# A four-stage residual chain on one core: n2 of blocks 1 to 6 turned in 32x32 squares by VectorE and moved by DMA, L3 two steps back

## The chip, the core and the metric

The kernel runs on one core of a Trainium2 chip: TensorE (matmul), VectorE, ScalarE, GpSimd and the sync engine SP, which issues nearly all DMAs. A core has SBUF (128 partitions) and PSUM (8 banks of 128 x 512 fp32, here pt 0 and 1, pc 0 and 1, pm 0 to 3). The metric is device time in microseconds.

## The reference

x is (2, 2048, 512) fp32. Four layers follow each other; the weights of the last three are picked by an index for each of the two sequences. Cut to what matters:

```python
# L0: gated traces, then a layer norm, residual
ctx = causal_ema(x, tau_ctx)
gated = x * sigmoid([x, ctx] @ Wg.T + bg)
...
n = layernorm((gelu(x @ Wsoma.T) * sigmoid(temporal @ Wtemp.T)) @ Wout.T) * gamma + beta
y = x + n
# L1: residual linear, per sequence
x2 = y + (y @ W[cat] + b)
# L2: adapter, then a layer norm, residual
x2' = x2 + relu(x2 @ W1[lang] + b1) @ W2[lang] + b2
x3 = x2 + layernorm(x2') * gamma2 + beta2
# L3: per-subject linear
out = x3 @ weight[subj].T + bias[subj]
```

## The kernel before, in words

The 4096 tokens are cut into 8 blocks of 512 (NBLK = 8, LAST = 7; blocks 0 to 3 are sequence 0, 4 to 7 sequence 1). Activations are mostly held channels by tokens, as 4 chunks (NC) of 128 x 512. fp32 products are made of three fp32r matmuls of a high and a low part (product(), L609 to L611), so each activation that enters a product is written twice: the high part by ScalarE (x_h, s_h, t_h, h_h), the rest by VectorE (x_l, s_l, t_l, h_l).

The first half of the time runs L0 over the 8 blocks; its normalised output n goes to n_scratch in DRAM, x to xt_scratch. There 16-bit pieces are transposed by DMA into x_pairs and put in order by four DMAs of 256 KB, x_pairs to x_planes (spread(), L290). The second half runs L1 to L3. A step step2(i) on TensorE (from L896), with nothing but the order of the code and semaphores as its plan:

- l1_product(i, m), m = 0 to 3: 12 matmuls each into pc; m = 2 needs x2_hi and x2_lo of m = 0 (the bank), m = 3 those of m = 1.
- inside m = 1 and m = 2 lie turn_n2(i-1): 16 transposes of stage_a (128x128, four fill a bank, turn(), L616), from tokens by channels into pt, channels by tokens.
- in steps 5 and 6 turn_y(i+1), 16 transposes of x_pairs.
- l3_product(i-1, k), k = 0 to 3: L3 of the block before, 12 matmuls each; w1_product(i) behind k = 0, xx_product(i) (4 tiles: x2 turned by 4 transposes, and 3 matmuls of the adapter) behind k = 2, k = 3 last.

What the other engines do for block i: ScalarE x2_parts (s_h and x_t from pc), relu_part, normalise of tiles 0 and 1 into stage_a, x2_beta (soma = x_t + beta_b2), x3_hi_part (t_h), y_hi_part (x_h). VectorE x2_lo_part (s_l, L1601), norm2_stats (L1632, L1635), normalise of tiles 2 and 3 (L1640), x3_sum_part (gate = n2 * gamma + soma from PSUM, L1610), x3_lo_part (t_l, L1616), y_sum_part (L1453), y_lo_part (x_l, L1594), hid_lo_part (L1621), output (L1628). GpSimd norm2_scale: rstd and nbias from the statistics (L503 to L519), and the low parts of two weights. SP load_y (n half into x_pairs, L392, xt half into ctx_t, L396) and store_out (L410). SP and each engine run strictly in order.

The names the prediction's steps touch: step2 and last_step2 on TensorE, l1_product, turn_n2, l3_bank, n2_bank; between the halves hid_lo_part(0), xx_product(0), turn_l3(1, k) and subject_lo(1, k) (wt_l, L1589), which make the L3 weights of sequence 1.

Of the kernel before, what the change touches and what calls it, by code (L numbers as in the profile page):

```python
# [5 lines left out]
P = 128  # L6
# [16 lines left out]
def residual_chain_kernel(nc: bass.Bass, t: dict, out: bass.AP):  # L23
# [23 lines left out]
    with ExitStack() as ctx:  # L47
# [3 lines left out]
        def sem(name):  # L51
# [106 lines left out]
        (y_hi, x2_hi, x2_all, relu_done, hid_hi, n2_act, n2_dve, x3_hi) = (  # L158
            sem(n) for n in ("y_hi", "x2_hi", "x2_all", "relu_done", "hid_hi", "n2_act", "n2_dve", "x3_hi"))
# [24 lines left out]
        l2_raw = [mod[:, :, :], stage_b[:, 0:2, :]]  # L184
# [10 lines left out]
        def x2_parts_of(i):  # L195

            return (t_h, t_l) if isinstance(i, int) and i == 0 else (s_h, s_l)
# [41 lines left out]
        def last_block(j):  # L239
            return isinstance(j, int) and j == LAST  # L240
# [4 lines left out]
        def first_block(j):  # L245
            return isinstance(j, int) and j == 0

        def n2_bank(j, c):
            if last_block(j):
                return [pc[0], pc[1], pt[1], pt[0]][c]  # L250
            return [pt[0], pt[1], pm[2], pm[3]][c] if first_block(j) else pt[c % 2]

        def l1_bank(i, m):

            return pc[(m + 1) % 2] if isinstance(i, int) and i == 1 else pc[m % 2]

        def l3_bank(j, k):
            if isinstance(j, int) and j == NBLK - 2:
                return [pm[0], pm[1], pt[1], pt[0]][k]
            return [pm[0], pm[1], pm[2], pm[3] if last_block(j) else pt[0]][k]  # L260
# [6 lines left out]
        def _(sp):  # L267
# [130 lines left out]
            def load_y(i):  # L398

                sp.wait_ge(y_sum, i * NC)  # L400
# [50 lines left out]
            load_l1_half(1, 1)  # L451
            store_n(LAST)
# [6 lines left out]
            def second_l2():  # L459
                sp.wait_ge(l3_turned, 2 * NC)  # L460
                load_l2(1)

            def store_block(j):
# [17 lines left out]
        def _(pool):  # L481
# [103 lines left out]
            def adapter_lo(b):  # L585
                for n, (raw, wh, wl) in enumerate(adapter_parts(b)):
# [17 lines left out]
        def _(pe):  # L604
# [209 lines left out]
            def l1_product(i, b, m, between=None):  # L814
# [14 lines left out]
                if between:  # L829
                    between()  # L830
# [953 lines left out]
```

## Time and profile before

| | |
|---|---|
| median of 3 runs | 757.39 us (757.36 to 757.73) |
| the profiled execution, its own time | 755.23 us |
| its span, first to last instruction | 753.3 us |
| instructions | 10450 |
| ScalarE busy | 366.7 us, 49% |
| GpSimd busy | 113.4 us, 15% |
| TensorE weight loads (beside matmuls) | 606.2 us, 80% |
| granted TensorE clock | 0.999 of full |
| DMA traffic | 86.17 MB, mean 114 GB/s |

Lines of the trace's timeline have: start in us, duration in us, engine, line of the kernel, operation, output <- inputs, shapes, count, and in brackets the idle time of the engine before it with what ended it. Matmuls are pipelined: a 128x512 matmul shows 0.39 us, but the next starts 0.23 later; the distance of starts is the price. The steps step2(i) lie from about 513 us to the end.

### The profile page before, as it was taken

What the parts mean: (1) busy time and instruction counts of PE and PEld (TensorE: products, weight loads), DVE (VectorE), ACT (ScalarE), POOL (GpSimd) and SP (SyncE); (2) the same over time, 40 slices, a digit from 0 to 9 for tenths busy, and PEclk for the clock granted to TensorE, in tenths of its full rate; (3) what the DMA queues carried; (4) which work ended last, traced back from release to release, by engine and by line L of the source; (5) the groups of instructions that cost most, each with busy time, mean ns of one, the idle gap of its engine ahead of it and who ended that gap; (6) DMA issues with size and microseconds to landing.
All of it is one profiled execution on the core that took longest, in us unless ns stands there. A gap on an engine that the chain in (4) does not pass through costs nothing. (4 is left out here: it accounts for less than half of the span.)

```text
span 753.3 us, 10450 instructions
## 1 busy us (share of the span) xinstructions
PE 743.6 (99%) x3421; PEld 606.2 (80%) x3421; DVE 534.3 (71%) x786; ACT 366.7 (49%) x550; POOL 113.4 (15%) x222
## 2 busy tenths in 40 slices
PE   7999999999999999999999999999999999999997
PEld 6888888888888888888888788878888888888885
DVE  4598895695695595597587579866867767666645
ACT  5363346445535535535536543656564553636331
POOL 2000040031022013004004024114301021010110
PEclk9999999999999999999999999999999999999999
DMA  8964007916934953962971872526143131331002
GB/s 267 222 180 45 28 1 110 195 59 97 188 78 79 189 95 65 185 111 54 169 139 31 138 223 73 207 85 220 56 157 138 57 127 55 129 107 74 28 33 80
DMA packets 93020, 86.17 MB, mean 114 GB/s; under 512 B 61583, under 2 KB 75950, under 8 KB 90942
## 3 DMA queue, kind: packets, MB, share of 16 engines
q1 hardware_dynamic: 91614, 81.57, 45.2%
q10 hardware_dynamic: 1184, 4.23, 1.7%
q8 instruction: 15, 0.25, 0.1%
q0 software_dynamic: 192, 0.00, 0.1%
q14 instruction: 15, 0.12, 0.1%
HBM read 33.33 MB, written 25.20 MB: 78 GB/s over the span
## 5 line engine op out<-in xcount | busy, mean ns | idle before, releaser
L609 PE MATMUL pc<-x_h,wg_h 128*128 128x512 f32 x224 | 88.8, 396 | 0.0
L611 PE MATMUL pc<-x_h,wg_l 128*128 128x512 f32 x224 | 88.1, 393 | 0.0
L610 PE MATMUL pc<-x_l,wg_h 128*128 128x512 f32 x224 | 87.7, 391 | 0.0
L1421 DVE TENSOR_TENSOR_SCAN stage_b<-alpha,carry,stage_b 128x512 f32<-128x512 f32 x64 | 78.5, 1268 | 0.0
L1100 ACT ACTIVATE ctx_t<-ctx_t,col_all 128x512 f32<-128x512 f32 x32 | 23.1, 723 | 57.1 <-DVE ctx_t L1401 57.1
L609 PE MATMUL pm<-wo_h,s_h 128*128 128x512 f32 x128 | 50.7, 396 | 0.0
L611 PE MATMUL pm<-wo_h,s_l 128*128 128x512 f32 x128 | 50.6, 395 | 0.0
L610 PE MATMUL pm<-wo_l,s_h 128*128 128x512 f32 x128 | 50.6, 395 | 0.0
L726 PE MATMUL pm<-t_h,wt_l 128*128 128x512 f32 x128 | 50.6, 395 | 0.0
L724 PE MATMUL pm<-t_h,wt_h 128*128 128x512 f32 x128 | 50.5, 395 | 0.0
L725 PE MATMUL pm<-t_l,wt_h 128*128 128x512 f32 x128 | 50.3, 393 | 0.0
L609 PEld LDWEIGHTS pc<-x_h,wg_h 128*128 128x128 f32 x224 | 42.2, 188 | 9.8 <-issue 0.6
L611 PEld LDWEIGHTS pc<-x_h,wg_l 128*128 128x128 f32 x224 | 42.1, 188 | 9.4
L610 PEld LDWEIGHTS pc<-x_l,wg_h 128*128 128x128 f32 x224 | 42.1, 188 | 9.1
L503 POOL TENSOR_TENSOR newton<-mv,const 128x4 f32<-128x4 f32 x16 | 9.6, 600 | 251.5 <-DVE mv L1635 181.1
L1415 DVE SCALAR_TENSOR_TENSOR stage_b<-mod,w_blend,ctx_t 128x512 f32<-128x512 f32 x64 | 45.7, 756 | 2.4 <-DVE ctx_t L1405 1.5
L1374 DVE SCALAR_TENSOR_TENSOR gate<-gate,soma 128x512 f32<-128x512 f32 x32 | 21.9, 698 | 35.6 <-ACT gate L1055 35.6
L1106 ACT ACTIVATE t_h<-stage_b 128x512 fp32r<-128x512 f32 x32 | 20.4, 636 | 47.9 <-DVE stage_b L1428 47.7
L1055 ACT ACTIVATE gate<-pm,col_all 128x512 f32<-128x512 f32 x32 | 21.6, 688 | 45.2 <-PE pm L726 29.9
L1256 ACT ACTIVATE stage_a<-pm,nbias,rstd 128x512 f32<-128x512 f32 x16 | 11.6, 775 | 55.9 <-POOL nbias L519 55.8
L1601 DVE SCALAR_TENSOR_TENSOR s_l<-pc,seq_b,s_h 128x512 fp32r<-128x512 f32 x28 | 21.0, 750 | 24.0 <-ACT x_t L1231 24.0
L611 PE MATMUL pc<-x_h,ws_l 128*128 128x512 f32 x96 | 38.0, 396 | 0.0
(245 smaller groups left out, 1932.7 us busy)
## 6 DMA issues: line engine op xcount, KB each, us to landing
x_planes<-x_pairs SPq DMA_DIRECT2D x52, 256.0 KB, 7.4
xt_scratch<-x_t SPq DMA_DIRECT2D x8, 1024.0 KB, 10.3
n_scratch<-stage_a SPq DMA_DIRECT2D x8, 1024.0 KB, 10.1
ctx_t<-xt_scratch SPq DMA_DIRECT2D x16, 512.0 KB, 6.3
x_pairs<-n_scratch SPq DMA_DIRECT2D x14, 512.0 KB, 5.3
out_dram<-x_tok SPq DMA_DIRECT2D x28, 256.0 KB, 2.0
mod<-mod_scratch ACTq DMA_DIRECT2D x8, 512.0 KB, 3.8
stage_b<-in_L_cond_weight_dram SPq DMA_DIRECT2D x2, 1024.0 KB, 5.5
```

The costliest lines, as they stand in the source:

```text
L609: nc.tensor.matmul(acc, ah, bh, start=start and q == 0, stop=False)
L610: nc.tensor.matmul(acc, ah, bl, start=False, stop=False)
L611: last = nc.tensor.matmul(acc, al, bh, start=False, stop=stop and q == n - 1)
L724: nc.tensor.matmul(pm[m][:, :], wt_h[:, c, o], t_h[:, c, :], start=(c == 0), stop=False)
L725: nc.tensor.matmul(pm[m][:, :], wt_h[:, c, o], t_l[:, c, :], start=False, stop=False)
L726: last = nc.tensor.matmul(pm[m][:, :], wt_l[:, c, o], t_h[:, c, :], start=False, stop=(c == NC - 1))
L1055: nc.scalar.activation(gate[:, m % 2, :], pm[m][:, :], ACT.Tanh, bias=cols["btemp"][:, m:m + 1], scale=0.5).then_inc(gate_t, 1)
L1100: nc.scalar.activation(ctx_t[:, m, :], ctx_t[:, m, :], ACT.Tanh, bias=cols["bg"][:, m:m + 1], scale=0.5).then_inc(z_t, 1)
L1374: nc.vector.scalar_tensor_tensor(gate[:, m % 2, :], gate[:, m % 2, :], 1.0, soma[:, m, :], ALU.add, ALU.mult).then_inc(s_prod, 1)
L1415: nc.vector.scalar_tensor_tensor(tr[:, m % 2, :], mod[:, d, :], w_blend[:, d, m:m + 1], ctx_t[:, m, :], ALU.mult, ALU.mult).then_inc(prods, 1)
L1421: nc.vector.tensor_tensor_scan(tr[:, m % 2, :], alpha[:, 1 + d:2 + d].to_broadcast([P, BLK]), tr[:, m % 2, :], carry[:, D - d, m:m + 1], A ...
L1601: nc.vector.scalar_tensor_tensor(c_l[:, m, :], l1_bank(i, m)[:, :], seq["b1"][:, b, m:m + 1], f32(c_h[:, m, :]), ALU.add, ALU.subtract).th ...
```

## The change

n2 of blocks 1 to 6 is no longer transposed by TensorE. ScalarE normalises all four tiles of such a block into stage_a, VectorE transposes 32x32 squares within each (turn_squares) into stage_b, SP moves the squares by 16 DMAs of 64 KB between groups of 32 partitions into x_planes (move_n2), ScalarE applies gamma and beta and puts the columns in order (scale_n2), VectorE adds x2 (x3_sum_part). That takes longer from end to end, so L3 of block j runs in step j + 2 and not j + 1, with other banks; x2 alternates between x_t and soma, and x2_beta goes. Blocks 0 and 7 are still turned by TensorE. Step 1 and step 2 are written out on their own, the tail (last_blocks) has L3 of block 6 around turn_n2(7). The loops over steps are unrolled. VectorE's order within a step is new. The load of y of block 2 comes before store_n(LAST), and VectorE sums it ahead of hid_lo(0). adapter_lo(1) moves from GpSimd to VectorE.

```diff
+        def turned_by_pe(j):
+
+
+            return j == 0 or j == LAST
+
+        def n2_acts(j):
+
+            return 2 + 4 * j - (2 if j == LAST else 0)
...
+            def move_n2(j):
+
+                sp.wait_ge(n2_squares, j * TILES)
+                if j == 1:
+                    sp.wait_ge(x3_lo, NC)
+                else:
+                    sp.wait_ge(n2_scaled, (j - 1) * NC)
+                for q in range(4):
+                    for a in range(4):
+                        part, tok = slice(32 * a, 32 * a + 32), slice(P * a, P * a + P)
+                        sp.dma_start(x_planes[32 * q:32 * q + 32, :, tok],
+                                     squares_q[part, :, q, :]).then_inc(n2_in, 16)
...
+            second_l3()
+            sp.wait_ge(s_lo, NBLK * NC)
+            load_l2(1)
+            store_out(0, 0)
+            load_y(3)
+            store_out(0, 1)
+            for i in range(2, NBLK):
+                move_n2(i - 1)
+                if i == 2:
+                    load_y(4)
+                    store_out(0, 2)
+                    store_out(0, 3)
+                    continue
+                store_out(i - 2, 0)
+                store_out(i - 2, 1)
+                if i + 2 < NBLK:
+                    load_y(i + 2)
+                store_out(i - 2, 2)
+                store_out(i - 2, 3)
+            for j in (LAST - 1, LAST):
                 for k in range(TILES):
                     store_out(j, k)
-
-            load_y(2)
-            second_l3()
-            store_block(0)
-            second_l2()
-            with sp.Fori(2, LAST) as i:
-                load_y(i + 1)
-                store_block(i - 1)
-            store_block(LAST - 1)
-            store_block(LAST)
...
+            def second_step2():
+                for m in range(NC):
+                    if m < 2:
+                        pe.wait_ge(l3_hi, 2 * NC)
+                        pe.wait_ge(l3_lo, 2 * NC)
+                    l1_product(2, 0, m)
+                l3_tile(0, 2)
+                w1_product(2, 0)
+                l3_tile(0, 3)
+                for k in range(TILES):
+                    xx_product(2, 0, k)
+
+            def step2(i):
+                b = i // PER_SEQ
+                l1_product(i, b, 0)
+                l1_product(i, b, 1)
+                if turns_y(i):
                     turn_y(i + 1, 0)
                     turn_y(i + 1, 1)
-                if not weights:
-                    l3_product(i - 1, bp, 0)
-                    w1_product(i, b)
-                if turned:
+                l1_product(i, b, 2)
+                l1_product(i, b, 3)
+                if turns_y(i):
                     turn_y(i + 1, 2)
-                l3_product(i - 1, bp, 1)
-                if turned:
                     turn_y(i + 1, 3)
-                l3_product(i - 1, bp, 2)
-                if weights:
-                    pe.wait_ge(relu_done, i + 1)
-                    turn_l3(1, 0, pt[1])
-                    turn_l3(1, 1, pc[1])
+                l3_tile(i - 2, 0)
+                w1_product(i, b)
+                l3_tile(i - 2, 1)
+                l3_tile(i - 2, 2)
                 for k in range(TILES):
                     xx_product(i, b, k)
-                if weights:
-                    turn_l3(1, 2, pt[1])
-                    turn_l3(1, 3, pc[1])
-                l3_product(i - 1, bp, 3, turned)
-
-            def last_step2(i, b):
-                l1_product(i, b, 0)
-                l1_product(i, b, 1, lambda: turn_n2(i - 1, (0, 1)))
-                l1_product(i, b, 2, lambda: turn_n2(i - 1, (2, 3)))
-                l1_product(i, b, 3)
-                l3_product(i - 1, b, 0)
-                w1_product(i, b)
-                l3_product(i - 1, b, 1)
-                for k in range(TILES):
-                    xx_product(i, b, k)
-                pe.wait_ge(x3_sum, i * NC)
-                l3_tile(l3_bank(i - 1, 2), b, 2)
-                l3_tile(l3_bank(i - 1, 3), b, 3)
-                turn_n2(i, range(NC))
-
-                wh, wl = l3_w(b)
+                l3_tile(i - 2, 3)
+
+            def last_blocks():
+                l3_tile(LAST - 1, 0)
+                l3_tile(LAST - 1, 1)
+                turn_n2(LAST)
+                l3_tile(LAST - 1, 2)
+                l3_tile(LAST - 1, 3)
...
+            def scale_n2(j, m):
+
+                b = j // PER_SEQ
+                act.wait_ge(n2_in, j * 256)
+                nc.scalar.activation(stage_b[:, m, :].rearrange("p (k a i) -> p k a i", k=TILES, a=4),
+                                     x_planes[:, m, :].rearrange("p (a k i) -> p k a i", k=TILES, a=4), ACT.Identity,
+                                     bias=seq["beta_b2"][:, b, m:m + 1],
+                                     scale=seq["gamma2"][:, b, m:m + 1]).then_inc(n2_scaled, 1)
+
...
+            def turn_squares(j, k):
+
+                dve.wait_ge(n2_act, n2_acts(j - 1) + k + 1)
+                if j == 1:
+                    dve.wait_ge(l3_turned, 2 * NC)
                 else:
-                    x2_lo_part(i, b, 0)
-                    x3_sum_part(i - 1, bp, 0)
-                    x3_sum_part(i - 1, bp, 1)
-                    x3_lo_part(i - 1, 0)
-                    x3_lo_part(i - 1, 1)
-                    x2_lo_part(i, b, 1)
-                    x3_sum_part(i - 1, bp, 2)
-                    x3_sum_part(i - 1, bp, 3)
-                    x3_lo_part(i - 1, 2)
-                    x3_lo_part(i - 1, 3)
-                    x2_lo_part(i, b, 2)
-                    x2_lo_part(i, b, 3)
-                if not last:
-                    y_sum_part(i + 1, 0, turned)
-                    y_sum_part(i + 1, 1, turned)
-                    y_lo_part(i + 1, 0)
-                    y_lo_part(i + 1, 1)
-                output(i - 1, bp, 0)
+                    dve.wait_ge(x3_lo, j * NC)
+                nc.vector.transpose(squares[:, :, k, :], stage_a[:, k, :].rearrange("p (f i) -> p f i", i=32)
+                                    ).then_inc(n2_squares, 1)
+
+            def adapter_lo(b):
+                for n, (raw, wh, wl) in enumerate(adapter_parts(b)):
+                    dve.wait_ge(l2_hi, b * 2 + n + 1)
+                    nc.vector.tensor_tensor(wl, raw, f32(wh), ALU.subtract).then_inc(l2_lo, 1)
+
+            def step2(i):
+                j = i - 2
+                turned, more = turns_y(i), i < LAST
+                if j >= 1:
+                    for m in range(NC):
+                        x3_lo_part(j, m)
+                x2_lo_part(i, 0)
+                turn_squares(i - 1, 0)
+                if more and not turned:
+                    y_sum_part(i + 1, 0)
+                x2_lo_part(i, 1)
+                if more and not turned:
+                    y_sum_part(i + 1, 1)
+                    y_sum_part(i + 1, 2)
+                if turned:
+                    y_sum_part(i + 1, 0, True)
+                    y_sum_part(i + 1, 1, True)
+                turn_squares(i - 1, 1)
+                turn_squares(i - 1, 2)
+                x2_lo_part(i, 2)
+                turn_squares(i - 1, 3)
+                if more and not turned:
+                    y_sum_part(i + 1, 3)
+                x2_lo_part(i, 3)
+                if turned:
+                    y_sum_part(i + 1, 2, True)
+                    y_sum_part(i + 1, 3, True)
+                if more:
+                    for c in range(NC):
+                        y_lo_part(i + 1, c)
+                output(j, 2 if j == 0 else 0)
                 hid_lo_part(i)
-                if not last:
-                    y_sum_part(i + 1, 2, turned)
-                output(i - 1, bp, 1)
-                if not last:
-                    y_sum_part(i + 1, 3, turned)
-                    y_lo_part(i + 1, 2)
-                    y_lo_part(i + 1, 3)
-                    output(i - 1, bp, 2)
-                if weights:
-                    subject_lo(1, 0, pt[1])
-                    subject_lo(1, 1, pc[1])
+                output(j, 3 if j == 0 else 1)
+                if i == LAST:
+                    for m in range(NC):
+                        x3_sum_part(i - 1, m)
+                if j > 0:
+                    output(j, 2)
                 for k in range(TILES):
                     norm2_stats(i, k)
-                if weights:
-                    subject_lo(1, 2, pt[1])
-                    subject_lo(1, 3, pc[1])
-                if last:
-                    output(i - 1, bp, 2)
+                if i < LAST:
+                    for m in range(NC):
+                        x3_sum_part(i - 1, m)
                 else:
-                    output(i - 1, bp, 3)
-                normalise(i, 2)
-                normalise(i, 3)
-                if last:
-                    output(i - 1, bp, 3)
+                    for m in range(NC):
+                        x3_lo_part(i - 1, m)
+                if j > 0:
+                    output(j, 3)
 
...
+            for c in range(3):
+                y_sum_part(2, c)
             hid_lo_part(0)
```

## Rows read from the trace of the kernel before

**Rows 1.** Page, part 1: busy time, share of span, instructions.
```profile
PE 743.6 (99%) x3421; PEld 606.2 (80%) x3421; DVE 534.3 (71%) x786; ACT 366.7 (49%) x550; POOL 113.4 (15%) x222
```

**Rows 2.** TensorE's waits, whole span: us in total, times, longest.
```profile
PE pm L959 <- DVE t_l L1616: 1.1, 1, 1.1
```

**Rows 3.** Stretches: length, busy us by engine, TensorE clock, DMA share, GB/s.
```profile
611.50:642.80 31.30, 31.30 (x154) 25.77 (x153) 22.72 (x36) 15.70 (x25) 4.88 (x11) 1.00 0.29 99
642.80:675.85 33.05, 33.05 (x171) 27.41 (x170) 22.22 (x37) 15.42 (x24) 2.47 (x9) 1.00 0.27 99
```

**Rows 4.** Timeline of TensorE around one pair of n2 quads.
```profile
642.01 1.03 PE L616 MATMUL pt<-ident,stage_a 128*128 128x128 f32 x8
642.80 0.48 PE L609 MATMUL pc<-x_h,wo_h 128*128 128x512 f32 x1
643.12 0.39 PE L610 MATMUL pc<-x_l,wo_h 128*128 128x512 f32 x1
643.35 0.40 PE L611 MATMUL pc<-x_h,wo_l 128*128 128x512 f32 x1
```

**Rows 5.** Timeline of TensorE and VectorE, block 7's n2 and L3.
```profile
735.57 1.07 PE L616 MATMUL pc<-ident,stage_a 128*128 128x128 f32 x8
...
738.65 0.47 PE L959 MATMUL pm<-wt_h,t_h 128*128 128x512 f32 x1 [1.14 <-DVE t_l L1616]
...
737.81 0.69 DVE L1616 TENSOR_TENSOR t_l<-gate,t_h 128x512 fp32r<-128x512 f32 x1 [0.17 <-ACT t_h L1243]
```

**Rows 6.** VectorE: a group by line (busy, mean ns), and a pair in time.
```profile
L1421 DVE TENSOR_TENSOR_SCAN stage_b<-alpha,carry,stage_b 128x512 f32<-128x512 f32 x64 | 78.5, 1268 | 0.0
...
524.14 1.28 DVE L1616 TENSOR_TENSOR t_l<-gate,t_h 128x512 fp32r<-128x512 f32 x2
```

**Rows 7.** Timeline: end of xx(7), last statistics on VectorE, last scale on GpSimd.
```profile
729.71 0.40 PE L609 MATMUL pt<-wt_h,t_h 128*128 128x512 f32 x1
...
730.75 0.18 DVE L1635 BATCH_NORM_AGGREGATE mv<-stats 128x2 f32<-128x6 f32 x1
...
733.66 0.20 POOL L519 TENSOR_TENSOR nbias<-newton,nbias 128x4 f32<-128x4 f32 x1
```

**Rows 8.** Timeline of a tile of l1: TensorE, ScalarE, VectorE (step 1, m = 1).
```profile
513.26 0.40 PE L609 MATMUL pc<-x_h,wg_h 128*128 128x512 f32 x1
...
516.22 0.69 ACT L1228 ACTIVATE s_h<-pc,seq_b 128x512 fp32r<-128x512 f32 x1 [2.08 <-PE pc L611]
...
517.62 0.75 DVE L1601 SCALAR_TENSOR_TENSOR s_l<-pc,seq_b,s_h 128x512 fp32r<-128x512 f32 x1 [2.46 <-ACT x_t L1231]
```

**Rows 9.** SP's issues in time, landing of x_planes, stretches during a spread.
```profile
299.51 2.61 SPq L290 DMA_DIRECT2D x_planes<-x_pairs  x4
...
310.05 4.60 SPq L284 DMA_TRANSPOSE x_pairs<-in_x_dram  x1
...
671.97 0.33 SPq L410 DMA_DIRECT2D out_dram<-x_tok  x1
...
DMA to landing us min/median/max: 4.4/7.4/9.3
...
303.00:304.00 1.00, 1.00 (x6) 0.82 (x5) 0.22 (x1) 0.69 (x2) 0.00 (x0) 1.00 1.17 123
...
310.00:311.00 1.00, 1.00 (x6) 0.51 (x5) 0.89 (x2) 0.00 (x0) 0.00 (x0) 1.00 1.03 434
```

**Rows 10.** Between the halves: SP, VectorE, TensorE; landing of ctx_t (L396).
```profile
497.21 0.95 SPq L373 DMA_DIRECT2D stage_b<-in_L_cond_W_dram  x2
...
498.18 2.73 DVE L1594 SCALAR_TENSOR_TENSOR x_l<-ctx_t,col_all,x_h 128x512 fp32r<-128x512 f32 x4
...
506.88 0.69 DVE L1621 TENSOR_TENSOR h_l<-h,h_h 128x512 fp32r<-128x512 f32 x1 [2.53 <-ACT h_h L1251]
...
508.64 0.66 PE L616 MATMUL pm<-ident,x_t 128*128 128x128 f32 x4 [0.40 <-ACT stage_a L1112]
...
DMA to landing us min/median/max: 3.8/6.3/8.3
```

More of the change, by code:

```diff
@@ L861, in xx_product @@
+                nc.tensor.matmul(pm[k][:, :], hl, wh, start=False, stop=False, skip_group_check=True)
+                nc.tensor.matmul(pm[k][:, :], hh, wl, start=False, stop=True,
                                  skip_group_check=True).then_inc(xx_mm, 1)
[L863 to L874 removed]
@@ new lines, in l3_tile @@
+            def l3_tile(j, k):
+                b = j // PER_SEQ
+                if turns_y(j + 2) and k < 3:
+                    pe.wait_ge(n2_act, n2_acts(j + 1))
+                elif turns_y(j + 2):
+                    pe.wait_ge(y_sum, (j + 3) * NC + 3)
+                elif j == LAST - 1 and k >= 2:
+                    pe.wait_ge(n2_act, n2_acts(LAST))
+                    pe.wait_ge(n2_dve, 4)
+                elif j == LAST - 1 and k == 0:
+                    pe.wait_ge(out_ready, j * TILES - 1)
+                else:
+                    after(pe, out_ready, j * TILES + max(k - 1, 0))
@@ new lines, in l3_tile, with first_step2 @@
+                for c in range(NC):
+                    if k == 0:
+                        pe.wait_ge(x3_hi, j * NC + c + 1)
+                        pe.wait_ge(x3_lo, j * NC + c + 1)
+                    last = product(l3_bank(j, k)[:, :], [(ch[:, c, tok], cl[:, c, tok], wh[:, c, :], wl[:, c, :])],
+                                   start=(c == 0), stop=(c == NC - 1))
+                last.then_inc(l3_mm, 1)
+            def first_step2():
+                for m in range(1, NC):
+                    l1_product(1, 0, m)
+                turn_n2(0)
+                w1_product(1, 0)
+                pe.wait_ge(l3_hi, NC)
+                pe.wait_ge(l3_lo, NC)
+                l3_tile(0, 0)
+                l3_tile(0, 1)
+                pe.wait_ge(relu_done, 2)
+                turn_l3(1, 0, pc[0])
+                turn_l3(1, 1, pc[1])
+                for k in range(TILES):
+                    xx_product(1, 0, k)
+                turn_l3(1, 2, pc[0])
+                turn_l3(1, 3, pc[1])
@@ new lines, in step2 @@
+            def step2(i):
+                if i >= 3:
+                    for m in range(NC):
+                        x3_hi_part(i - 2, m)
+                x2_parts(i, 0)
+                normalise(i - 1, 0)
+                x2_parts(i, 1)
+                normalise(i - 1, 1)
+                normalise(i - 1, 2)
+                x2_parts(i, 2)
+                normalise(i - 1, 3)
+                x2_parts(i, 3)
+                if i < LAST:
+                    for c in range(NC):
+                        y_hi_part(i + 1, c)
+                relu_part(i)
+                for m in range(NC):
+                    scale_n2(i - 1, m)
@@ L1313, in _ @@
             subject_hi(0, 3, pt[1])
[L1314 to L1316 removed]
+            relu_part(0)
             for k in range(TILES):
@@ new lines, in _ @@
+            x3_lo_part(0, 0)
+            x3_lo_part(0, 1)
+            x3_sum_part(0, 2)
+            x3_sum_part(0, 3)
+            x3_lo_part(0, 2)
+            x3_lo_part(0, 3)
+            hid_lo_part(1)
+            for c in range(NC):
+                y_lo_part(2, c)
+            output(0, 0)
+            output(0, 1)
+            subject_lo(1, 0, pc[0])
+            subject_lo(1, 1, pc[1])
+            for k in range(TILES):
+                norm2_stats(1, k)
+            subject_lo(1, 2, pc[0])
@@ L1747, in _ @@
+            subject_lo(1, 3, pc[1])
+            adapter_lo(1)
+            for i in range(2, NBLK):
+                step2(i)
+            normalise(LAST, 2)
+            normalise(LAST, 3)
+            output(LAST - 1, 0)
+            output(LAST - 1, 1)
+            x3_sum_part(LAST, 0)
+            x3_sum_part(LAST, 1)
             x3_lo_part(LAST, 0)
-            x3_sum_part(LAST, 1, 2)
+            x3_sum_part(LAST, 2)
             x3_lo_part(LAST, 1)
-            x3_sum_part(LAST, 1, 3)
+            x3_sum_part(LAST, 3)
```

391 lines of the change are left out of this document (158 added, 233 removed).

## Prediction, made before the change was built

> **What bounds the kernel now.** I read the totals of the page first: TensorE is busy for 99% of the span, VectorE for 71% [rows 1]. A share alone doesn't prove a bound, so TensorE's waits come next: in the second half the longest is 1.1 us, in front of the last L3 [rows 2], and the next 0.4 [rows 10]. The table of stretches then shows one step of the second half as 31.3 us, TensorE busy throughout at the full granted clock, and 33.05 us where 16 more transposes (turn_y) lie in the step [rows 3]. So in the second half every TensorE instruction that goes shortens the kernel, as long as nothing else becomes late. Every other engine matters only through the moment at which TensorE needs its result.
>
> **What is removed from TensorE.** turn_n2 of blocks 1 to 6: 16 transposes a block, in two pairs of quads inside l1_product. One pair in the timeline: transposes from 642.01, next matmul 642.80, the second one 643.12, then the ordinary pitch of 0.23 [rows 4]. Without the transposes that second matmul would come 0.23 after 642.01 and not 1.11: eight transposes cost 0.88 us, a block 1.76, six blocks 10.6. The step with 16 more of them is 1.7 longer [rows 3], which gives 10.3 for six. I take 10.5. The rest of TensorE's work stays (l1, w1, xx, L3, turn_y), only L3 is moved.
>
> **The tail.** Today the 16 transposes of block 7 begin at 735.57, take 1.8, and L3 starts at 738.65, behind x3_lo(7,0): about 1.2 us idle [rows 5]. After, two L3 tiles of block 6 stand in front of turn_n2(7) and two behind it (12 matmuls x 0.23 = 2.8 us each). x3_lo(7,0) is ready some 3 us after turn_n2 started, L3 of block 7 begins 1.8 + 5.6 after it. 1.2 us gained.
>
> **Prices on the other engines.** Back to back, VectorE takes 0.60 us for a two-operand 128x512 and 0.66 for a three-operand one (a pair in 1.28, four in 2.73) [rows 6, 10]. Statistics end 1.2 us after xx (xx ends at 729.71, the last aggregate at 730.93), rstd and nbias 2.9 behind them (733.86) [rows 7]. A result of VectorE reaches TensorE 0.15 after its end (738.50 to 738.65) [rows 5]. The square transpose does not occur here. Its ends are the plain operation, 0.60, and the scan, the slowest 128x512 row there is, 1.27 [rows 6]; one operand in and one out is nearest to the plain one: 0.65. By the Trainium skill (DVE Microarchitecture Reference, section 3.8) a transpose sustains one element per cycle and lane; no row here can show it, and by it the price would stay at the lower end.
> VectorE in a steady step: x3_lo, outputs, x3_sum 12 x 0.60, hid_lo 0.6, x2_lo, y_sum, y_lo 12 x 0.66, statistics 4 x 0.95, squares 4 x 0.65: 22.1 us (24.6 with 1.27), against a TensorE step of 29.5 (31.3 - 1.8). Enough by the sum; the order decides. ScalarE loses x2_beta and gets scale_n2 (0.7 each) and two more normalise: some 18 us.
>
> **The order in a steady step (3 to 7), 0 = start of l1(i,0).** The statistics of i-1 end at -1.6 (the last L3 tile covers 2.8). x3_sum runs until 0.9, the output until 1.5, x3_lo(i-2) until 3.9. A finished l1 tile reaches ScalarE 2.96 after its start, x2_lo starts at 4.4 and ends at 5.1 [rows 8]. TensorE wants it for l1(i,2) at 5.5, less 0.15: 0.25 us of margin. Before x2_lo(i,1) stand a square and a y_sum (5.1 + 0.65 + 0.66 = 6.4); ScalarE hands over at 7.0, behind one normalise; done 7.8, wanted 8.1: 0.3 us, and the square may cost 1.27 before that slips. x2_lo 2 and 3 are wanted only by w1, at 13.8 and 15.9, and are done by 11.5 and 13.5. So a steady step should have no gap, narrowly; the squares are done at 12.3.
>
> **The move.** 16 DMAs of 64 KB, 2,048 runs of 512 B, SBUF to SBUF. Nearest: the four spreads of phase 1, also 1 MB from SBUF to SBUF, in runs of 1 KB: issued from 299.51, and the transfer that waits for them goes at 310.05, 10.5 us later, at 123 GB/s [rows 9]. SP needs 0.33 for the issue of a 128-row store and 0.65 for a spread [rows 9], so 5.3 to 10.4 us in all. Lower end 9.7: issue 5.3 and the shortest landing, 4.4 [rows 9]. Upper end 19: at 123 GB/s a packet of 1 KB takes 133 ns on its engine; if one of 512 B took as long, 128 an engine are 17, and 2 to land. I take 10.5, since bytes, path and partitions are those of the spread. Then n2 is there at 22.8, scale_n2 ends at 25.4, x3_sum starts at 27.9 by its place behind the statistics: hidden, and the cover reaches from 12.3 to 27.2. SP's queue: store_out(i-2,0), (i-2,1) and load_y(i+2) stand behind the move; the issue ends by 18 to 23, the outputs come at 17.5 and 20.2, the loads land 6.3 us after their issue [rows 10], near 29, and y_sum wants them at 5.7 of the next step. Nothing late.
>
> **Four new waits** (no row of before has them; each is placed by the prices above).
> 1. *Between the halves.* y_sum(2, 0 to 2) now stands before hid_lo(0), which has 2.5 us of idle time in front of it today. Its ctx half can be issued only after y_lo(1), 500.9, and lands 3.8 to 8.3 us after 501.3 [rows 10]: 505.1 to 509.6. I take 506.5, behind 2 MB issued from 497.2. Three sums and hid_lo end at 509.3, TensorE goes on at 509.4 and not at 508.64 [rows 10]: 0.8 us (0 to 3.5).
> 2. *Into step 2.* turn_l3(1,2) and (1,3) now use pc, and l1(2,0) follows at once, where an L3 tile of 2.8 us stood between. It waits for subject_lo(1,3): statistics at xx + 1.2, two of 0.6, signal: xx + 2.6; TensorE would be there at xx + 0.88. 1.75 us (0.9 to 2.5).
> 3. *Into step 3.* No L3 tile stands behind xx(2), so x3_sum(1) and x3_lo(1) run while TensorE is at l1(3,0): 1.2 + 2.4 + 2.4 = 6.0, x2_lo(3,0) until 6.75, signal 6.9, against 5.5: 1.4 us (0.9 to 2).
> 4. *Last step.* x3_sum(6) stands before the statistics of block 7 and waits for move and scale. Squares 11.5 + 10.5 = 22.0, x3_sum until 25.1, output 25.7, statistics 29.4, x3_lo(6,0) 30.1; l3(6,0) wants it at 29.3: 0.8 (0 with a move of 9.7; each us more costs one).
>
> **Sum.** -10.5 - 1.2 + 0.8 + 1.75 + 1.4 + 0.8 = -7.0 us. The profiled execution took 755.23 (span 753.3 and 1.9 around it) and would take 748.2; the median of the runs, 757.39, is 2.16 above it, so the forecast for the median is 750.4.
>
> **Rivals.**
> A. *The move is far too long: slower than before.* Place: n2_scaled in front of x3_sum. At the upper end, 19 us, step 2 has x3_sum(1) at 32.2 instead of 25.2: +7. From there the loop of squares, move, scale, x3_sum, x3_lo, x2_lo is 5.8 + 19.2 + 6.9 = 31.9 us against 29.5: +2.4 in each of four steps, and the last adds about 4. +20 us: 770. It decides from a move of about 15 us on. For it: packets half as long, pieces from 32 partitions into 32. Against it: the spreads run at 123 GB/s where the store right behind them runs at 434 [rows 9], so what limits them looks like the bytes between partitions, which stay the same. Chance 0.10.
> A2. *The issue on SP paces the move:* 16 x 0.65 = 10.4 and 4.4 to land, 14.8 us. Step 2 loses 2.6, the last step 4.3 more: 757.3, no change. For it: sixteen pieces where before has four. Against it: the 0.33 of a 128-row issue. Chance 0.07. The Trainium skill (DMA: Bandwidth & Descriptors, section Bandwidth) calls transfers under 64 KB dominated by descriptors and has 0.95 us for 64 KB; sixteen in a row would be 15.2, an estimate from that page close to this rival. Its paragraph on small descriptors says that SBUF to SBUF doesn't suffer from them, which speaks for the forecast. No row here has such a piece.
> B. *The margins of 0.25 and 0.3 don't hold.* Squares over 1.3 us or slower hand-overs cost 0.5 to 0.9 in each of five or six steps: +3 to +5, 754.5. For it: the margins are as thin as my readings are sure. Against it: today's steps run the same hand-over without a gap [rows 3, 8]. Chance 0.18.
> C. *The new waits are smaller.* Block 2 lands at 505, the move takes 9.7: waits 1 and 4 vanish, 748.8; with all four gone the floor is 757.4 - 11.7 = 745.7. Chance 0.15.
> D. *The transposes were hidden anyway.* Rows 3 and 4 exclude it: 16 more lengthen a step by their full price.
> The forecast itself (749 to 753) has 0.50.
>
> **Range and chances.** Nearly down to the floor, 746.5, and up through B and A2 to 757.5; A and a little at both ends stay out, so it holds about 0.8. A measurement of this kernel can tell 0.2% (1.5 us) from no change: faster is under 755.9. Faster: 0.50 + 0.15 + 0.15 of B = 0.80; same: 0.03 of B and 0.05 of A2, 0.08; slower: A and 0.02 of A2, 0.12.
>
> **What would show it.** Right: 96 fewer transposes on stage_a; steps of 29.5 (31.3 with turn_y); TensorE's waits are l1(2,0) on wt_l, 1.7, l1(3,2) on s_l, 1.4, and none in steps 4 to 6; the last block's L3 starts without one. The mean of the square transpose and the time from the first x_planes issue to scale_n2 (under 12) decide between forecast, A, A2 and B. Wrong: a wait for s_l in every step, or VectorE's x3_sum behind scaled n2 in the middle steps.

## The result: slower by 0.4%, and the profile after

| | before | after |
|---|---|---|
| median | 757.31 us (755.0 to 757.73, 11 runs) | 760.47 us (755.8 to 763.65, 11 runs) |
| profiled execution, its own time | 755.23 us | 760.47 us |
| its span | 753.3 us | 758.7 us |
| granted TensorE clock | 0.999 | 0.991 |

The ratio of the times is 1.0042, interval 1.0023 to 1.0062. The forecast was 750.4 us with a range up to 757.5: wrong in sign. The runs of after differ in their mean TensorE clock, and their times go roughly with it: the one at 0.998 took 755.8 us, the two at 0.995 took 758.1 and 758.3, the four at 0.993 took 758.8 to 762.6, the four at 0.991 took 760.5 to 763.7.

Two things on comparing. The profiled executions, from which all lines come, differ by 5.2 us and the medians by 3.2: the profiled execution of before is near the fastest of its runs, that of after is the median. And each experiment's ratio is to executions of before taken along with it, whose medians were 755.73 us (experiments 1 to 4) and 756.3 (5 to 8), where the table has 757.31. So ratios can be compared with each other, medians can't.

The page of after, totals, answers to [rows 1]:

```profile
span 758.7 us, 10088 instructions
...
PE 738.8 (97%) x3325; PEld 599.2 (79%) x3325; DVE 534.4 (70%) x800; ACT 369.9 (49%) x554; POOL 124.0 (16%) x220
```

3421 - 3325 = 96 transposes are gone from TensorE. It is busy for 4.8 us less (743.6 and 738.8) while the span grew by 5.4: it stands idle for 10.2 us more. TensorE's waits (total, times, longest) answer to [rows 2]:

```profile
PE pm L653 <- DVE h_l L1664: 5.1, 1, 5.1
PE pt L653 <- DMA x_tok<-in_x_dram: 3.5, 1, 3.5
PE pc L646 <- DVE s_l L1632: 2.4, 1, 2.4
PE pt L646 <- DVE s_l L1659: 2.3, 1, 2.3
PE pc L646 <- ACT wt_h L1242: 1.6, 1, 1.6
...
PE pt L646 <- DVE t_l L1655: 0.4, 1, 0.4
```

The second one lies at the very start, where the first x is loaded. The other four long ones are the four new waits of the prediction; before has nothing above 1.1 in its second half [rows 2]. Their places on TensorE's timeline, from four stretches of it:

```profile
513.87 1.08 PE L653 MATMUL pm<-ident,x_t 128*128 128x128 f32 x4 [5.09 <-DVE h_l L1664]
...
515.17 0.63 PE L891 MATMUL pm<-ws_h,h_l 128*128 128x512 f32 x1
515.60 0.63 PE L892 MATMUL pm<-ws_l,h_h 128*128 128x512 f32 x1
...
547.32 0.47 PE L646 MATMUL pc<-x_h,wg_h 128*128 128x512 f32 x1 [1.62 <-ACT wt_h L1242]
547.62 0.39 PE L647 MATMUL pc<-x_l,wg_h 128*128 128x512 f32 x1
547.86 0.39 PE L648 MATMUL pc<-x_h,wg_l 128*128 128x512 f32 x1
...
579.40 0.77 PE L646 MATMUL pc<-x_h,wg_h 128*128 128x512 f32 x1 [2.39 <-DVE s_l L1632]
...
580.39 0.63 PE L648 MATMUL pc<-x_h,wg_l 128*128 128x512 f32 x1
580.82 0.63 PE L646 MATMUL pc<-x_h,wg_h 128*128 128x512 f32 x1
...
729.58 0.76 PE L646 MATMUL pt<-wt_h,s_h 128*128 128x512 f32 x1 [2.30 <-DVE s_l L1659]
...
730.57 0.63 PE L648 MATMUL pt<-wt_h,s_l 128*128 128x512 f32 x1
731.00 0.63 PE L646 MATMUL pt<-wt_h,s_h 128*128 128x512 f32 x1
```

Look at the durations and distances, not only at the brackets. Behind the wait of 1.62 the matmuls show 0.39 and start 0.23 apart. Behind the other three they show 0.63 and start 0.43 apart: after those waits TensorE runs at the lower of its two clocks, 1.2 GHz, until it returns to 2.4. The table of stretches says it with the granted clock, 1.00 for 2.4 GHz and 0.50 for 1.2 (columns: stretch, length, busy us of TensorE, its weight loads, VectorE, ScalarE and GpSimd, granted clock, DMA share, GB/s):

```profile
510.00:511.00 1.00, 0.00 (x0) 0.00 (x0) 0.00 (x0) 1.00 (x3) 0.00 (x0) 0.95 0.07 20
511.00:512.00 1.00, 0.00 (x0) 0.00 (x0) 0.96 (x2) 1.00 (x3) 0.00 (x0) 0.50 0.61 254
...
515.00:520.00 5.00, 5.00 (x23) 4.07 (x23) 2.45 (x5) 0.00 (x0) 0.00 (x0) 0.73 0.00 0
...
580.00:585.00 5.00, 5.00 (x18) 3.99 (x17) 3.95 (x6) 2.63 (x5) 0.00 (x0) 0.74 0.10 36
...
605.02:634.75 29.73, 29.73 (x137) 24.04 (x136) 21.41 (x37) 16.77 (x26) 4.90 (x10) 1.00 0.48 140
634.75:666.30 31.55, 31.51 (x153) 25.69 (x152) 23.08 (x40) 17.03 (x26) 6.33 (x12) 1.00 0.50 150
...
730.00:735.00 5.00, 5.00 (x17) 3.91 (x17) 3.77 (x7) 1.45 (x2) 2.65 (x8) 0.72 0.14 52
```

In the first two rows TensorE is idle: the clock fell there, inside the wait, some 3 us before the first matmul behind it. The two stretches of the middle are step 4 and step 5 (with turn_y) and answer to [rows 3]: 31.3 became 29.7 and 33.05 became 31.55, at the full clock.

**The account**, from the starts of the same groups of matmuls in both traces: xx_product(0) starts 4.65 us later behind the start of l1_product(1, 0), and itself takes 6.38 us and not 4.62 (1.76 of slow clock); into step 2 +1.78; l1 of step 3 takes 15.13 and not 11.03 (2.4 of waiting, 1.7 of slow clock); the 36 matmuls of L3 before the last transposes take 12.39 and not 8.40 (2.3 and 1.7); 0.6 was lost ahead of the seam. Against it stand 10.2 us for the six blocks of transposes (1.5 to 1.8 a block) and 1.4 at the tail. 0.6 + 6.4 + 1.8 + 4.1 + 4.0 - 10.2 - 1.4 = +5.3, of 5.4 measured. Two of these terms belong to this execution more than to the kernel. The 0.6: in the traces of the experiments the same l1_product(1, 0) starts anywhere from 505.1 to 509.5 us, though none changes TensorE's work ahead of it. And the 4.1 of step 3: in experiments 1, 6 and 7, which leave that step as it is, its l1 takes 12.85 to 12.96 us, with a wait of 1.6 to 1.7 and no slow matmul.

So four questions: is the wait between the halves made by the early y_sum(2), and why is it so long; what makes the waits in step 3 and the last step; is the slow clock a result of the waits; and is everything else of the change a gain.

### The profile page after: what moved, and what is told of

Same layout as the page of the kernel before. It is cut to its first block, busy times and chain, and to the rows that moved or that the text cites. A ratio compares the mean times of both kernels' runs of the same rounds, so it can differ in the third digit from the quotient of the medians.

```text
span 758.7 us, 10088 instructions
## 1 busy us (share of the span) xinstructions
PE 738.8 (97%) x3325; PEld 599.2 (79%) x3325; DVE 534.4 (70%) x800; ACT 369.9 (49%) x554; POOL 124.0 (16%) x220
## 4 chain that ended last, share of the span: by engine, by line
PE 89%; DVE 3%; SPq 3%; DMA 2%; issue 2%; ACT 1%; DVEq 0%; ACTq 0%
PE pc L646 12%; PE pc L648 11%; PE pc L647 11%; PE pt L646 7%; PE pt L648 7%; PE pt L647 7%; PE pm L647 5%; PE pm L648 5%; PE pm L646 5%; PE pm L763 4%; PE pm L761 4%; PE pm L762 4%; PE pm L653 3%; SPq L448 3%; DMA ctx_t<-xt_scratch 1%
## 5 line engine op out<-in xcount | busy, mean ns | idle before, releaser
L548 POOL TENSOR_TENSOR newton<-mv,const 128x4 f32<-128x4 f32 x16 | 11.5, 721 | 243.9 <-DVE mv L1678 171.9
L646 PE MATMUL pc<-x_h,ws_h 128*128 128x512 f32 x96 | 37.9, 395 | 0.0
L647 PE MATMUL pc<-x_l,ws_h 128*128 128x512 f32 x96 | 37.8, 394 | 0.0
## 6 DMA issues: line engine op xcount, KB each, us to landing
xt_scratch<-x_t SPq DMA_DIRECT2D x8, 1024.0 KB, 10.2
```

The source lines that it names most:

```text
L646: nc.tensor.matmul(acc, ah, bh, start=start and q == 0, stop=False)
L647: nc.tensor.matmul(acc, ah, bl, start=False, stop=False)
```

## Experiments

Theory W: the change of the transposes is worth its 10 us; the waits, above all that of y_sum(2) before hid_lo(0), and the slow clock behind them take it away. Rivals: the loss comes from the move itself (its DMA traffic, the queue on SP), or from VectorE's new load, and would stay if the order were mended. Diffs are against the kernel after where nothing else is said.

**1. The sums of block 2 behind x2_lo(1,0).**

```diff
-            for c in range(3):
-                y_sum_part(2, c)
             hid_lo_part(0)
-            y_sum_part(2, 3)
             for k in range(TILES):
                 norm2_stats(0, k)
             x2_lo_part(1, 0)
+            for c in range(NC):
+                y_sum_part(2, c)
```

> The changed kernel with one edit: the four sums of y of block 2 go behind x2_lo(1,0) instead of in front of hid_lo(0); the early load stays. Theory W (the loss is four waits of TensorE, and behind the long ones its matmuls run at 0.43 instead of 0.23 us for a while): the wait of 5.1 us for h_l and the 1.8 us of slow matmuls behind it go, 6.4 us together, so 760.5 becomes about 754.1 (ratio to before 0.996), and the stretch behind xx(0) shows the full clock. Rival M (the squares, the move and the new order cost something in every step, the first wait is only where the slack is used up): the time taken out here comes back in later steps, under 2 us gained. Rival P (the clock is lower because the changed kernel as a whole draws more, not because TensorE stood still): the wait goes, but as many slow matmuls turn up elsewhere, about 756.

Measured: 753.63 us (750.95 to 756.05), ratio to before 0.9967 (0.9952 to 0.9981). The wait at 513 is gone, xx_product(0) takes 4.62 us. TensorE's waits:

```profile
PE pc L646 <- DVE s_l L1632: 2.6, 2, 1.6
PE pt L646 <- DVE s_l L1659: 2.3, 1, 2.3
PE pc L646 <- ACT wt_h L1242: 1.6, 1, 1.6
```

Against after that is 0.75%, or 5.7 us, of the 6.4 expected: the place of four instructions decides the sign of the whole change. The waits of 1.6 into step 2 and of 2.3 in the last step stay. No matmul in this trace is slow (mean clock 1.0), though the last wait is as long as in after; it is the fastest of the 12 executions, and others of the same kernel have clocks down to 0.995. The first line holds two waits: 1.60 in step 3 and 1.04 in step 4, where after loses only 0.2. Ahead of the second, VectorE stood for a store:

```profile
592.21 0.69 DVE L1670 TENSOR_TENSOR x_tok<-pt,mod 128x512 f32<-128x512 f32 x1 [5.39 <-DMA out_dram<-x_tok]
```

SP had issued that step's stores only at 589.84, behind the 16 issues of the move. The output waits for them, the statistics stand behind the output, and x3_sum, x3_lo and x2_lo behind these. So the move also reaches TensorE by way of SP's queue; this is the kind of cost that rival M had in mind, 1 us of it.

**2. A tile of L3 as cover in step 3.** l3_tile(0, 3) goes behind xx(2), as in the steps before the change.

```diff
                 w1_product(2, 0)
-                l3_tile(0, 3)
                 for k in range(TILES):
                     xx_product(2, 0, k)
+                l3_tile(0, 3)
```

> The changed kernel with one edit: L3 tile 3 of block 0 goes behind xx(2), its output behind x3_sum(1), as in the steps after it. Theory W: the wait of 2.4 us for s_l in step 3 and the 1.7 us of slow matmuls behind it go, 4.1 us together: about 756.4, l1 of step 3 takes 11.1 us instead of 15.1. Rival M: DVE is simply late with x3_lo and squares, and the wait only becomes 1 to 2 us shorter or moves to x2_lo(3,1) or step 4: 758 to 760. Rival P: the wait goes, the slow matmuls don't.

Measured: 760.28 us (758.19 to 761.63), ratio 1.0049 (1.0030 to 1.0069): no gain, a miss. The wait in step 3 shrank to 0.5, but there is a new one in front of xx(2):

```profile
565.86 0.63 PE L653 MATMUL pm<-ident,x_t 128*128 128x128 f32 x4 [2.21 <-ACT h_h L1289]
```

The tile had been the cover for relu and high part of the adapter's hidden values, which follow w1: 0.69 and 0.63 of ScalarE and their signals. I had only seen the hole that it left, not the one that it filled. And that hole was smaller than the 4.1 us expected: in experiments 1, 6 and 7, with step 3 as in after, its l1 takes 12.85 to 12.96 us. Here it takes 11.41, 1.5 less, and the new wait costs 2.2.

**3. Part of the move issued by ScalarE's queue.** Of the 16 pieces, 3 (in the last step 6) leave from ScalarE's queue, before relu_part.

```diff
-                for q in range(4):
-                    for a in range(4):
...
+                for n in range(16 - by_act(j)):
+                    move_piece(sp, n)
...
+                for n in range(16 - by_act(i - 1), 16):
+                    move_piece(act, n)
                 relu_part(i)
```

> The changed kernel with one edit: of the 16 pieces of each move ScalarE's queue issues 3 (6 for block 6) just ahead of relu_part, SP the rest. Theory W with SP's issue as the pace of the move (0.68 us a piece, 10.3 to 11.8 for 16, landing 2): the move of block 6 ends about 2.4 us earlier (10 pieces on SP), x3_sum(6) no longer holds up the statistics of block 7, the wait of 2.3 us on s_l in front of L3 of block 6 and the 1.7 us of slow matmuls go: about 756.5. Rival: the transfers themselves are the pace (packets of 512 B); then the move ends no earlier and the time stays at 760.5. Second rival: relu of a step comes late behind ScalarE's issues (0.7 us each) and TensorE waits for h_l in each step: slower than 760.5.

Measured: 753.47 us (752.93 to 756.98), ratio 0.9958 (0.9942 to 0.9975). The last move in after, SP and ScalarE, and then in this kernel:

```profile
709.13 10.26 SPq L448 DMA_DIRECT2D x_planes<-stage_b  x16
...
720.87 2.93 ACT L1277 ACTIVATE stage_b<-x_planes,seq_beta_b,seq_gamma 128x512 f32<-128x512 f32 x4 [5.15 <-DMA x_planes<-stage_b]
```

```profile
709.63 6.41 SPq L228 DMA_DIRECT2D x_planes<-stage_b  x10
...
710.26 3.50 ACTq L228 DMA_DIRECT2D x_planes<-stage_b  x5
...
717.52 2.94 ACT L1282 ACTIVATE stage_b<-x_planes,seq_beta_b,seq_gamma 128x512 f32<-128x512 f32 x4 [1.32 <-DMA x_planes<-stage_b]
```

From first issue to scale_n2: 11.7 us with 16 pieces in one queue, 7.9 with 10 in the longer one. 6 pieces x 0.64 = 3.8 us, just the difference. So the issue on SP, not the bytes, sets the length of the move. The stretch of the move in after says the same: the DMA engines are busy for 0.47 of it, at 100 GB/s, where the spread of [rows 9] kept them busy throughout at 123.

```profile
709.13:720.87 11.74, 11.74 (x54) 9.46 (x53) 2.83 (x4) 2.22 (x5) 0.00 (x0) 1.00 0.47 100
```

The 36 matmuls of L3 are back at 8.40 us without a wait, and l1 of step 3 takes 12.50 with a wait of 1.2: 4.0 + 2.6 = 6.6 us in these two places, 6.4 by the ratios, where 4.0 had been expected. The profiled execution as a whole is only 3.5 us shorter than that of after, because its l1_product(1, 0) starts at 509.48 and not 505.87: 3.6 us were lost ahead of everything that the edit touches. One trace's total would have misled here.

**4. All three, with two more covers.** turn_l3(1, 2) and (1, 3) go between the tiles of xx(1), their subject_lo between the statistics, so that L3's weights of sequence 1 come sooner. Beside the edits of 1, 2 and 3, on TensorE (and in the same way on VectorE):

```diff
-                for k in range(TILES):
-                    xx_product(1, 0, k)
+                xx_product(1, 0, 0)
+                xx_product(1, 0, 1)
                 turn_l3(1, 2, pc[0])
                 turn_l3(1, 3, pc[1])
+                xx_product(1, 0, 2)
+                xx_product(1, 0, 3)
```

> The changed kernel with the three edits of the other runs of this call, and a fourth: turn_l3(1, 2 and 3) go between xx(1,1) and xx(1,2), and subject_lo(1, 2 and 3) between the statistics of tiles 1 and 2, so that two tiles of xx cover them in front of l1(2,0). Theory W: 6.4 + 4.1 + 4.0 + 1.8 = 16.3 us go, 760.5 - 16.3 = 744.2 (ratio to before 0.983), which is what the removed transposes (10.5) and the tail (1.2) were worth by themselves, TensorE without a wait over 0.5 us behind the first load and the clock at 1.00 throughout. Rival M: the steady steps have costs that the four waits now hide; 748 or more. Rival P: clock still under 0.995, 748 or more.

Measured: 747.37 us (746.4 to 750.47), ratio 0.9889 (0.9868 to 0.9910), clock 1.0. The four waits are gone, that of experiment 2 is there with 2.2 us. By the profiled executions that wait is all that is missing: 746.4 measured, 744.2 expected. By the ratios 0.6%, or 4.5 us, is missing to the expected 0.983, and only half of it is explained.

**5. The kernel before, with the early sums alone.** Nothing of the transposes or of L3 is changed. Against the kernel before, on VectorE; on SP load_y(2) moves up to where the kernel after has it:

```diff
+            for c in range(3):
+                y_sum_part(2, c)
             hid_lo_part(0)
+            y_sum_part(2, 3)
```

> The kernel before with one part of the change alone: load_y(2) ahead of store_n(LAST), and y of block 2 summed in front of hid_lo(0) instead of in step 1. Theory W: the ctx half lands 9.4 us after its issue, VectorE stands in front of hid_lo(0), TensorE waits some 5 us in front of xx(0) and its matmuls behind the wait run at 0.43 us for a while: 6.4 us slower than before, ratio 1.0085. Rival: the 5 us belong to something else of the change (the new banks, L3 two steps back), then this kernel is within 1 us of before, and as VectorE has four sums less in step 1, perhaps 0.2 us faster.

Measured: 761.81 us (761.22 to 765.09), ratio 1.0077 (1.0054 to 1.0101). TensorE waits for hid_lo(0) and comes out slow, with nothing of the rest of the change in the kernel. Its longest wait, and then two stretches with the granted clock:

```profile
PE pm L616 <- DVE h_l L1621: 4.5, 1, 4.5
```

```profile
510.00:515.00 5.00, 1.90 (x7) 1.73 (x8) 3.34 (x5) 3.24 (x6) 0.00 (x0) 0.59 0.51 210
515.00:520.00 5.00, 5.00 (x24) 4.09 (x23) 2.64 (x6) 0.00 (x0) 0.00 (x0) 0.73 0.00 0
```

Up to the end of xx_product(0) that is 4.0 us of later start and 2.1 of slow matmuls. The rival that blames the move or VectorE's load can't explain this 0.77%.

**6. Filler in the first wait.** 20 matmuls without use stand in front of xx_product(0), so that TensorE is busy while it would wait.

```diff
+            pe.wait_ge(l3_hi, NC)
+            pe.wait_ge(l3_lo, NC)
+            for k in range(20):
+                nc.tensor.matmul(pt[0][:, :], wg_h[:, 0, 0:P], wg_h[:, 1, :], start=(k == 0), stop=(k == 19))
```

> The changed kernel with 20 matmuls of 128x512 without use (4.6 us, bank pt 0) in front of xx(0), where TensorE waits 5.1 us for h_l; nothing else. They add no wait, since they end before h_l is there. Theory W with a price of its own for the slow clock (xx(0) took 6.4 us where it takes 4.6): xx(0) takes 4.6 us and the kernel gets 1.8 us faster, 758.7, although TensorE has more to do. Rival: the slow matmuls come from something else (DMA traffic, the chip as a whole): xx(0) still 6.4, the time as it was.

Measured: 759.8 us (755.17 to 763.13), ratio 1.0026 (1.0004 to 1.0047); the interval overlaps that of after, so by the median the saving isn't shown. TensorE's timeline, and then the stretch:

```profile
510.33 4.72 PE L1019 MATMUL pt<-wg_h 128*128 128x512 f32 x20
515.44 0.63 PE L653 MATMUL pm<-ident,x_t 128*128 128x128 f32 x4 [0.40 <-DVE h_l L1668]
```

```profile
510.00:515.00 5.00, 5.00 (x23) 3.82 (x21) 2.38 (x4) 5.00 (x10) 1.45 (x4) 1.00 0.47 194
```

xx_product(0) waits as long for hid_lo(0) as before, but takes 4.60 us and not 6.38: 1.78 us. With TensorE busy in that place its clock did not fall, which was worth 1.8 us. The last step of this profiled run had a wait of 3.4 (2.3 in after) and was slow behind it (13.58 for the 36 matmuls), which hides the saving in its total. The reason lies in the move ahead of it:

```profile
707.10 11.37 SPq L448 DMA_DIRECT2D x_planes<-stage_b  x16
```

```profile
PE pt L646 <- DVE s_l L1663: 3.4, 1, 3.4
```

The 16 issues took 11.37 us and not 10.26, and the wait is longer by the same 1.1: at this place each us of the move is a us of TensorE's.

**7. The load of block 2 issued before the weights.** load_y(2) stands ahead of load_l1_half(1) in SP's order; VectorE's order is that of after.

```diff
+            load_y(2)
             load_l1_half(1, 0)
             load_l1_half(1, 1)
-            load_y(2)
```

> The changed kernel with load_y(2) in front of the two halves of load_l1(1) instead of behind them: 1 MB less in the queue ahead of ctx. Theory Q (the ctx half lands late because 2 MB stand before it in the queue): it lands 2.5 to 3 us earlier, near 508, and the wait for h_l shrinks from 5.1 to about 2.3 us; some slow matmuls go too: 757 or less. Rival D (reading xt_scratch or the write into ctx_t is slow by itself): the landing stays at 9.4 us after the issue, the time at 760. Rival C (the loads are taken from the DMA rings together, not one behind the other): SP now issues l1 behind the ctx half, so ctx still shares with it; landing earlier by 1 us at most.

Measured: 756.6 us (752.64 to 758.04), ratio 0.9999 (0.9982 to 1.0016). SP's issue of the ctx half and VectorE's first sum, in after and in this kernel:

```profile
501.56 0.98 SPq L422 DMA_DIRECT2D ctx_t<-xt_scratch  x2
...
511.04 2.08 DVE L1484 SCALAR_TENSOR_TENSOR ctx_t<-x_pairs,col_all,ctx_t 128x512 f32<-128x512 f32 x3 [6.10 <-DMA ctx_t<-xt_scratch]
513.03 0.68 DVE L1664 TENSOR_TENSOR h_l<-h,h_h 128x512 fp32r<-128x512 f32 x1
```

```profile
501.34 0.80 SPq L422 DMA_DIRECT2D ctx_t<-xt_scratch  x2
...
508.19 2.08 DVE L1484 SCALAR_TENSOR_TENSOR ctx_t<-x_pairs,col_all,ctx_t 128x512 f32<-128x512 f32 x3 [3.48 <-DMA ctx_t<-xt_scratch]
```

The issue can't move: ctx_t is free only after y_lo(1). But the sum starts 6.9 us behind it, not 9.5. The 2.6 us go with the weights (1 MB) that no longer stand ahead, more than the 1 us that rival C allowed. The wait is 2.71 us, xx_product(0) is at the full clock (4.59): 4.2 us in that place by the trace. By the ratios the kernel is 0.43% or 3.2 us faster than after, with intervals that don't overlap; 3.5 had been expected.

**8. As 4, with the tile in halves.** Two of the four chunks of l3_tile(0, 3) in front of xx(2), two behind.

```diff
+                l3_tile(0, 3, (0, 1))
                 for k in range(TILES):
                     xx_product(2, 0, k)
-                l3_tile(0, 3)
+                l3_tile(0, 3, (2, 3))
```

> As the run of all four edits, but L3 tile 3 of block 0 is cut: 6 matmuls in front of xx(2), 6 behind. There the whole tile behind xx(2) had moved the wait: TensorE stood 2.2 us in front of xx(2), behind w1 with no tile between, until relu and the high part of the hidden layer were done. Theory W: 1.4 us of cover in front leave 0.8 of the 2.2; 1.4 us behind are enough for x3 now that the move is shorter (that wait was 1.2 us with ScalarE's share): 1.4 us faster than that run, ratio to before 0.987. Rival: the second half is too little cover, 1 us comes back in step 3: no difference from that run, 0.989.

Measured: 747.3 us (745.85 to 748.68), ratio 0.9870 (0.9848 to 0.9893): the median is the 0.987 that was expected, but the intervals of 4 and 8 overlap, so the gain over 4 isn't shown. In the trace the wait of 2.2 is split into 0.81 in front of xx(2) and 0.39 in step 3. This is a version 1.3% faster than before and 1.7% faster than after.

## Why the prediction was wrong

**Right: the sum of what is removed.** TensorE was the bound, and 96 transposes gave 10.2 us of the 10.5 taken from [rows 3, 4]; the tail gave 1.4, where 1.2 had been read from [rows 5]. Rival D is out.

**Right: the places of all four new waits, and wait 2.** Into step 2: 1.78 measured, 1.75 worked out. A wait that could be built from prices of the trace, with no transfer in it, came out to 0.03 us.

**Right: the steady steps.** 29.7 and 31.55 us for 29.5 and 31.3. Rival B did not come: none of the margins of 0.25 and 0.3 cost more than a tenth or two. Start to start the square transpose took 0.62, for 0.65, and scale_n2 0.71, for 0.7. But the same step 4 lost 0.5 to 1.3 us in the traces of experiments 1, 2, 6 and 7 (l1 in 11.46 to 12.29 us, 11.0 without a wait), and nothing in those of 3, 4 and 8 with the shorter move. "Nothing late" for the stores behind the move was a step with too little margin; the trace of after happened to show 0.2 of it.

**Wrong: wait 1, by 3.8 us.** The step was "I take 506.5", from a range of 505.1 to 509.6 that I had laid out myself. It landed at 511, above even that end: 9.1 us from issue to landing by the profile (9.5 from the start of the first of the two issues), where [rows 10] has 8.3 as the longest. I had chosen a landing of 5 us, near the lower end, although I named the 2 MB issued ahead of it in the same sentence; experiment 7 prices half of these at 2.6 us. Stretches of after have the rate at which the queues were served:

```profile
501.00:506.00 5.00, 5.00 (x23) 4.08 (x22) 3.29 (x7) 0.51 (x2) 0.98 (x3) 1.00 0.93 290
...
508.60:511.04 2.44, 0.18 (x1) 0.00 (x0) 0.00 (x0) 2.44 (x5) 1.11 (x3) 0.97 0.11 40
```

At 290 GB/s, with the DMA engines 93% busy, the 3 MB (the 2 MB and ctx_t itself, 3.15 million bytes) take 10.8 us, from 497.8 to 508.6. The last 2.4 us before the landing are not the rate: the DMA engines are busy for 0.11 of them, at 40 GB/s. What the landing waited for there stays open. I had no row for either, and so the late end of the range was the value to take; with its 3.5 us wait 1 would still have been 1.1 short.

**Wrong: no term for the clock.** The sum priced a wait as its length. Three of the four were followed by matmuls at the lower clock, which cost about 1.7 us each: 5.2 us in all, as much as the longest wait. No row of before shows it, since before has no idle TensorE in its second half beyond 1.1 us; but as no row showed what follows a longer wait, the range should have reached higher for it.

**Wrong: waits 3 and 4, by 1.0 and 1.5 us.** The move was taken at 10.5 us from the spreads. It was 13.2 in step 2, 12.4 in the next, 11.7 in the last: 16 x 0.64 to 0.73 of issue (10.3 to 11.8) and 1.4 to 1.5 behind the last issue. What had made the spreads slow, the bytes between partitions, wasn't what limited it (experiment 3). Rival A2 had the right mechanism and even the right price of an issue, 0.65, taken from a spread of [rows 9]; it added 4.4 for a landing that takes 2.0. I gave it 0.07 since a 128-row store is issued in 0.33: the store was the wrong neighbour. The spread goes from SBUF to SBUF like the move, and its 0.65 was the right price. By the page of the Trainium skill cited there (DMA: Bandwidth & Descriptors, section Bandwidth) the estimate was 15.2; its 0.95 us for 64 KB is for a load from HBM issued by GpSimd. The trace is between that and my 10.5. In step 2 a second loss followed: x3_sum could not run at its own 0.60 each but followed scale_n2 one by one:

```profile
572.24 2.94 ACT L1277 ACTIVATE stage_b<-x_planes,seq_beta_b,seq_gamma 128x512 f32<-128x512 f32 x4 [6.70 <-DMA x_planes<-stage_b]
...
573.17 2.81 DVE L1646 TENSOR_TENSOR stage_b<-stage_b,soma 128x512 f32<-128x512 f32 x4 [0.60 <-ACT stage_b L1277]
575.89 2.49 DVE L1659 TENSOR_TENSOR t_l<-stage_b,t_h 128x512 fp32r<-128x512 f32 x4
578.51 0.75 DVE L1632 SCALAR_TENSOR_TENSOR s_l<-pc,seq_b,s_h 128x512 fp32r<-128x512 f32 x1
```

Statistics end at 572.56, x3_sum starts 0.6 later and takes 2.81 where it takes 2.50 in step 3, and x2_lo(3, 0), for which TensorE waits, stands at the end of this chain. That 0.9 is nearly the whole miss of wait 3: in experiments 1, 6 and 7, where the move of step 2 took 12.4 to 12.5 us, the wait is 1.60 to 1.70 for the 1.4 worked out. So the prediction had wait 3 nearly right, and the trace of after shows it with a long move. In the last step x3_sum again takes 2.81, behind a move of 11.7; by the prediction's own "each us more costs one" that move gives 2.0, of 2.3 measured.

**In numbers:** wait 1 +3.8, slow clock +5.2, waits 3 and 4 +2.5, ahead of the seam +0.6, transposes and tail +0.1, together 12.2: the profiled run was to take 748.2 and took 760.47. The floor of rival C, 745.7 for the median, is 743.5 for the profiled execution (755.23 - 11.7). Experiment 4, with none of the four waits but one of 2.2 us of its own, has 746.4 there.

## What to carry to other kernels

When an instruction is moved ahead of another on an in-order engine, its operand must be there by then: read when its transfer can be issued and how many bytes are ahead of it in the queues, and take the late end at least. A transfer in many pieces is also priced by its issues, 16 x 0.64 to 0.73 us here, and so is what stands behind them in that queue. A tile of matmuls taken out of one place covered something: name what it covered there before giving it to the next hole. Where TensorE has been without a gap, allow for a slow stretch behind a new wait of some 2 us or more, here 1.2 to 2.1 us in the executions that had it.

## What the runs showed of the hardware

- **The clock.** TensorE's granted clock fell to 1.2 GHz in waits of 5.1, 2.4 and 2.3 us (after) and 3.4 (experiment 6), at 1.7 to 1.8 us each, and in waits of 5.3 (experiment 2), 4.9 (experiment 3) and 4.5 (experiment 5), at 1.2, 1.9 and 2.1. It did not in waits of 2.3 (last step of experiments 1, 2 and 7), 2.2 (experiments 2 and 4) and 2.7 (experiment 7). So between 2.2 and 2.7 us the length of the wait alone doesn't decide; what else does stays open. It differs between executions of one kernel: the runs of after, whose mean clocks lie between 0.991 and 0.998, spread over 7.9 us; those of before, all at 0.999 to 1.0 where the clock is on record, over 2.7 to 3.8.
- **Issue.** A 64 KB piece from SBUF to SBUF costs its queue 0.64 to 0.73 us of issue and lands in 2.0 us (median); two queues issue side by side. The same 16 issues took from 10.25 to 11.8 us from one step and one execution to another; why is open.
- **The square transpose.** 24 instructions of 128x512 fp32 in 32x32 squares took 0.70 us each on VectorE, 0.62 from start to start; a plain two-operand addition (x3_sum) shows 0.69.
